# A DLRM tower on one core: ScalarE turns the ids of the first two halves into distances, VectorE compares them with constants, and the first ids are loaded ahead of the first table

## The chip, the core and the metric

The kernel runs on one core of a Trainium2 chip. The metric is the device time of a run in microseconds. The kernel before took 383.13 us (median of 3 runs, 382.71 to 384.81). What can be told about where that time goes comes from one profiled execution of the same program.

## The reference

For 2048 samples, 27 embedding rows of 128 floats are looked up, all pairs of the 27 are multiplied out, and a small network runs over the 351 dot products and 16 dense features.

```
e = stack([tbl_f[ids[:, f]] for f in range(27)], axis=1)       # 2048 x 27 x 128
dot = einsum('bnd,bmd->bnm', e, e)                             # 2048 x 27 x 27
z = dot at the 351 pairs i < j
h = concatenate([z, dense_ctx], axis=1)                        # 2048 x 367
h = maximum(h @ W_top1 + b_top1, 0)                            # 512 wide
h = maximum(h @ W_top2 + b_top2, 0)                            # 256 wide
y = h @ W_top3
```

The tables have 1000 to 125000 rows. Ten of the small ones (seven with 1000 rows, three with 1250) are read in a special way, below.

## The kernel before

**Tiles and halves.** The batch is cut into 16 tiles of 128 samples, and two neighbouring tiles make a half, so there are 8 halves (h = 0 to 7). For every tile the embeddings are needed turned, with the 128 numbers of a row on the partitions, in `embT`. There are two ways into `embT`.

**Gathered features.** GpSimd (POOL) issues one indirect DMA for each tile and feature (L379), which fetches 128 rows from the table into `emb` (three for the first two tiles into `flatT`). TensorE turns them four at a time (a "quad", L420, function `turn`) into a bank of PSUM, and ScalarE copies the bank to `embT` (`copy_quad`, L642). A tile has 20 gathered features in half 0 and 17 later, so five quads, written here as quad(t, q). There are 278 gathers in all, issued in one fixed order.

**Features read in one piece ("hots").** For the ten small tables the row is picked by a matrix product. A table lies in SBUF on 125 partitions, 8 or 10 rows (chunks) to a partition, so row r lies on partition r // c as chunk r % c, where c is 8 or 10. For each chunk VectorE builds a matrix `one_hot` of 125 x 256 zeros and ones (`build`, L537): it compares the 256 ids of a half, which were copied to all partitions as int32 (`ids`), with one number per partition, `row_of[p, chunk] = c*p + chunk`. TensorE multiplies the chunk of the table with it (`read_table`, L410) and sums over the chunks in a bank of PSUM; ScalarE copies that bank to `embT` (`copy_hot`, L634). The hots are numbered in the order of use: hot 0 to 6 are those of half 0, hot 7 to 16 those of half 1, then ten for every half, 77 in all. Each has 8 or 10 comparisons, so 658 in all; 142 of them belong to hots 0 to 16.

**The tables are split first.** A table goes into the product as a rounded part and a rest. ScalarE makes the rounded part (`split_high`, L622), and VectorE the rest (`split_low`, L522, signal `low_ready`). Tables 0 to 4 are staged in the space of `embT` for later tiles, tables 5 to 9 in the buffers `h1T`, `w2_sb` and `w1_sb` that the network's weights need later. Tables 5 and 6 are read unsplit in half 0. Tables 8 and 9 are loaded only when table 7's and 8's stage in `w1_sb` has been read by `split_low`, and the weights `W1` after table 9's.

**The queues.** Each engine runs its own list in order, and one that waits holds everything behind it. TensorE, VectorE and ScalarE all walk through one list `ORDER`. Around half 1 it reads: quad(1,0), dots of tile 0 (part 0), hot 7, quad(1,1), hot 8, quad(1,2), dots of tile 0 (part 1), hot 9, quad(1,3), hot 10, quad(1,4), hot 11, quad(2,0), dots of tile 1 (part 0), the turning of tile 0's pairs, hot 12, quad(2,1), hot 13, quad(2,2), dots of tile 1 (part 1), hot 14, quad(2,3), hot 15, quad(2,4), hot 16, quad(3,0), dots of tile 2 (L442). Three banks of PSUM go round for quads and hots: TensorE may write for one of them only when ScalarE has copied the one three places earlier (`bank_of`, waits on `embT_ready`). VectorE builds one hot ahead of TensorE's reading.

ScalarE's splits of tables 5 to 9 stand right ahead of its copies of hots 7, 8, 9, 11 and 13 (`SPLIT_AT`). VectorE's stand ahead of the build of the hot after it.

SyncE issues the loads. Four buffers `ids` go round, and the load of the ids of hot n waits until hot n-4 is built. The part of its list on which much rests here is this:

```
for n in range(EARLY, len(HOTS)):        # EARLY = 11
    load_ids(n)
    if n == EARLY:
        load_table(SHARED + 1)           # table 8: waits for low_ready 8 (table 7's)
    elif n == EARLY + 2:
        load_table(SHARED + 2)           # table 9: waits for low_ready 9 (table 8's)
        sp.wait_ge(hot_used, BEFORE[len(HOT0)])
        sp.dma_start(w2_sb...)
    elif n == EARLY + 5:
        sp.wait_ge(low_ready, O)         # then W1, W3 and b2
```

So the ids of hots 12 and 13 go out behind table 8, and those of hots 14, 15 and 16 behind table 9 and `W2`.

Of the kernel before, what the change touches and what calls it, by code (L numbers as in the profile page):

```python
# [6 lines left out]
F32 = mybir.dt.float32  # L7
# [45 lines left out]
def dlrm_tower(nc, dense, idx_rows, ids_hot, tables, w1, w2, b2, w3, y):  # L53
# [54 lines left out]
    def hots_of(h):  # L108

        return range(READ_IN_HALF[h])  # L110
# [65 lines left out]
        BEFORE.append(BEFORE[-1] + GROUPS[o])  # L176
    READ = {step: n for n, step in enumerate(HOTS)}

    EARLY = len(HOT0) + IDS

    SHARED = WHOLE + 2
# [4 lines left out]
    with ctx:  # L186
# [6 lines left out]
        def sem(name):  # L193
            return ctx.enter_context(nc.semaphore(name))
# [84 lines left out]
        staged = [sem(f"staged{o}") for o in range(O)]  # L279
        high_ready = sem("high_ready")  # L280
        low_ready = sem("low_ready")
        ids_loaded = [sem(f"ids_loaded{b}") for b in range(IDS)]
        hot_built = sem("hot_built")
        hot_used = sem("hot_used")
# [27 lines left out]
        @block.sync  # L312
        def _(sp):
            def load_ids(n):
                _, h, o = HOTS[n]
                if n >= IDS:

                    sp.wait_ge(hot_built, BEFORE[n - IDS + 1])
                src = ids_hot[o:o + 1, h * HN:(h + 1) * HN].to_broadcast([P, HN])
                sp.dma_start(ids[:, n % IDS, :], src).then_inc(ids_loaded[n % IDS], 16)  # L320

            def load_table(o):
                if o > SHARED:

                    sp.wait_ge(low_ready, o)
                rows = tables[ONE_HOT[o]].rearrange("(p c) d -> p (c d)", p=ROWS)
                for a, b in ((0, SPLIT), (SPLIT, ROWS)):
                    sp.dma_start(raw(o, a, b), rows[a:b, :]).then_inc(staged[o], 16)

            sp.dma_start(idx[:, 0, :], idx_rows[:, 0, :]).then_inc(idx_first, 16)  # L330
            for o in range(SHARED + 1):
                load_table(o)
                if o < len(HOT0):
                    load_ids(o)
                if o == 2:
                    sp.dma_start(idx[:, 1:T, :], idx_rows[:, 1:T, :]).then_inc(idx_rest, 16)
            for n in range(len(HOT0), EARLY):
                load_ids(n)
            sp.dma_start(dense_sb[:, :, :], dense).then_inc(dense_loaded, 16)
            for n in range(EARLY, len(HOTS)):  # L340
                load_ids(n)
                if n == EARLY:
                    load_table(SHARED + 1)
                elif n == EARLY + 2:
                    load_table(SHARED + 2)

                    sp.wait_ge(hot_used, BEFORE[len(HOT0)])
                    sp.dma_start(w2_sb[:, :, :], w2.rearrange("(k p) n -> p k n", p=P)).then_inc(weights_loaded, 16)
                elif n == EARLY + 5:

                    sp.wait_ge(low_ready, O)
                    sp.dma_start(w1_sb[0:KR, :, :], w1).then_inc(weights_loaded, 16)
                    sp.dma_start(w3_sb[:, :], w3.to_broadcast([P, H2])).then_inc(weights_loaded, 16)
                    sp.dma_start(b2_sb[:, :], b2.to_broadcast([P, H2])).then_inc(weights_loaded, 16)
            sp.wait_ge(y_in_rows, 1)
            sp.dma_start(y.rearrange("(t c) o -> t (c o)", c=TILE), h2[0:T, 0:TILE]).then_inc(y_stored, 16)
            sp.wait_ge(y_stored, 16)
# [161 lines left out]
        def _(dve):  # L519
# [7 lines left out]
            def build(n):  # L527
                _, _, o = HOTS[n]
                of = ids[0:ROWS, n % IDS, :]
                dve.wait_ge(ids_loaded[n % IDS], 16 * (n // IDS + 1))  # L530
                for i in range(GROUPS[o]):
                    k = BEFORE[n] + i
                    if k >= SLOTS:
                        dve.wait_ge(hot_used, k - SLOTS + 1)
                    for c in range(GROUP):
                        chunk = i * GROUP + c
                        done = dve.tensor_scalar(one_hot[0:ROWS, k % SLOTS, c, :], of,  # L537
                                                 row_of[0:ROWS, KINDS.index(CH[o]), chunk:chunk + 1], None,
                                                 ALU.is_equal)
                    done.then_inc(hot_built, 1)  # L540

            def place_dense(t):
# [75 lines left out]
        @block.scalar  # L618
        def _(act):
            def split_high(o):  # L620
                act.wait_ge(staged[o], 32)
                act.copy(tbl[0:ROWS, 0, AT[o]:AT[o + 1], :],  # L622
                         raw(o, 0, ROWS).rearrange("p (c d) -> p c d", d=D)).then_inc(high_ready, 1)

            def copy_hot(h, o):
                n = READ["hot", h, o]
                if h == 1:

                    act.wait_ge(low_ready, WHOLE)
                elif h > 1:  # L630
                    act.wait_ge(dotted, PARTS * HT * (h - 1))
                act.wait_ge(hot_used, BEFORE[n + 1])
                at = h % 2 * HT
                act.copy(embT_at(at, HT, slot(o), 1),  # L634
                         embT_ps[USE["hot", h, o] % BANKS][:, 0:HN].rearrange("p (t s q) -> p t s q", t=HT, s=SIDES),
                         ).then_inc(embT_ready, 1)

            def copy_quad(t, q):
                s = quad(t, q)
                n = len(s)  # L640
                act.wait_ge(turned, TURNED["quad", t, q])
                act.copy(embT_at(t % TB, 1, s[0], n),  # L642
                         embT_ps[USE["quad", t, q] % BANKS][:, 0:n * P].rearrange("p (f s q) -> p f s q", f=n, s=SIDES),
                         ).then_inc(embT_ready, 1)

            def copy_ring(t):

                act.wait_ge(flat_filled, 4 * t + 2)
                if t >= 2:
                    act.wait_ge(flat_turned, t - 1)  # L650
                act.copy(pairs[:, t % 2, :, 1:HALF + 1], ring()).then_inc(first_pairs, 1)  # L651

            def copy_flat(t):
                act.wait_ge(flat_turned, t + 1)
                act.copy(flatT[0:KR, :, t % HT * TILE:(t % HT + 1) * TILE],  # L655
                         flat_ps[0:KR, 0:KC * TILE].rearrange("p (k c) -> p k c", k=KC)).then_inc(flatT_ready, 1)

            def relu1(n):
                act.wait_ge(h1_summed, n + 1)
                if n == T - 1:  # L660
                    at = n % HT * TILE
                    half = C1 // 2
                    act.activation(h1T[:, 0:half, at:at + TILE],
                                   h1_ps[:, 0:half * TILE].rearrange("p (k c) -> p k c", k=half),
                                   ACT.Relu).then_inc(h1_ready, 1)
                    act.wait_ge(h1_summed, n + 2)
                    act.activation(h1T[:, half:C1, at:at + TILE],
                                   flat_ps[:, 0:half * TILE].rearrange("p (k c) -> p k c", k=half),
                                   ACT.Relu).then_inc(h1_ready, 1)
                elif n >= T - HT:  # L670
                    act.activation(h1T[:, :, n % HT * TILE:(n % HT + 1) * TILE],
                                   h1_ps[:, :].rearrange("p (k c) -> p k c", k=C1), ACT.Relu).then_inc(h1_ready, 1)
                else:
                    first = n % HT * C1 // HT
                    act.activation(h1T[:, first:first + C1 // HT, :],  # L675
                                   h1_ps[:, :].rearrange("p (k c) -> p k c", k=C1 // HT),
                                   ACT.Relu).then_inc(h1_ready, 1)

            AHEAD = 3
            for o in range(AHEAD):  # L680
                split_high(o)
            for kind, *of in ORDER:
                if kind == "hot":
                    n = READ["hot", of[0], of[1]]
                    if n + AHEAD < WHOLE:
                        split_high(n + AHEAD)
                    elif n in SPLIT_AT:
                        split_high(SPLIT_AT[n])
                if kind == "quad":
                    copy_quad(*of)  # L690
                elif kind == "hot":
                    copy_hot(*of)
                elif kind == "ring":
                    copy_ring(*of)
                elif kind == "flat":
                    copy_flat(*of)
                elif kind == "layer1":
                    relu1(*of)
# [32 lines left out]
```

## Time and profile before

| | us |
|---|---|
| median of 3 runs | 383.13 (382.71 to 384.81) |
| the profiled execution, its time | 381.17 |
| its span, first to last instruction | 379.3 |
| TensorE busy | 345.7 |
| VectorE busy | 294.4 |
| GpSimd busy | 269.3 |
| ScalarE busy | 153.3 |

The span is shorter than the execution's time by 1.9 us, which lie around it. The profiled execution is 1.96 us shorter than the median. In what follows, PE is TensorE's matmuls, PEld its loads of weights, DVE is VectorE, ACT is ScalarE, POOL is GpSimd and SP is SyncE. Buffer numbers are left out of the names, so `w_sb` is `w1_sb` or `w2_sb`.

### The profile page before, as it was taken

Reading aid. Unit: us, or ns where it says so; the run is one execution under the profiler, and the core shown is the slowest. Engines: PE = TensorE matmul, PEld = TensorE weight load, DVE = VectorE, ACT = ScalarE, POOL = GpSimd, SP = SyncE. Lnnn points to the kernel's source line nnn. Section 1 sums busy time; section 2 is a strip of 40 time slices with the busy share of each in tenths; the row PEclk is TensorE's granted clock in tenths of the full one; section 3 lists DMA queues with packets and bytes.
Section 4 is the critical chain, followed back from the end, with each engine's and each line's share of the span. In section 5 each row is a group of like instructions: output and inputs, shape, how many; then the busy total and the mean of one; then the engine's idle time right before and its main releaser. Section 6 shows DMA issues by size and latency. Waiting matters only on the chain.

```text
span 379.3 us, 9954 instructions
## 1 busy us (share of the span) xinstructions
PE 345.7 (91%) x4035; PEld 322.6 (85%) x4035; DVE 294.4 (78%) x821; ACT 153.3 (40%) x217; POOL 269.3 (71%) x287
## 2 busy tenths in 40 slices
PE   1788868599999999999999999999999999999985
PEld 1677767588999999998999999998999999998874
DVE  4986696898688969798689969798689869793432
ACT  3352644434343453534343453534243453533421
POOL 6777877777777777777777777777777777777400
PEclk9989996999999999999999999999999999999999
DMA  6995225953333333334333333333343343221100
GB/s 184 251 247 136 64 63 137 213 186 96 82 93 85 79 84 82 95 69 95 82 94 85 79 86 81 95 72 91 85 91 85 76 89 83 76 57 50 36 2 1
DMA packets 22988, 36.38 MB, mean 96 GB/s; under 512 B 6224, under 2 KB 17120, under 8 KB 22944
## 3 DMA queue, kind: packets, MB, share of 16 engines
q0 software_dynamic: 8896, 18.24, 20.2%
q1 hardware_dynamic: 14048, 17.52, 18.6%
q8 instruction: 32, 0.52, 0.5%
q14 instruction: 12, 0.10, 0.1%
HBM read 35.73 MB, written 0.01 MB: 94 GB/s over the span
## 4 chain that ended last, share of the span: by engine, by line
PE 75%; POOL 14%; issue 5%; DMA 3%; ACT 2%; DVE 1%; ACTq 0%; DVEq 0%
PE embT_ps L410 35%; PE gram_ps L442 13%; POOL emb L379 12%; PE h_ps L470 11%; PE h_ps L494 7%; PE embT_ps L420 6%; DMA emb<-in_tbl,idx 3%; PE flat_ps L453 2%; POOL flatT L379 2%; ACT embT L634 1%; DVE flat L568 1%; DMA idx<-in_idx_rows 0%; PE h_ps L481 0%; PE flat_ps L481 0%; DVE flat L569 0%
## 5 line engine op out<-in xcount | busy, mean ns | idle before, releaser
L379 POOL DMA_INDIRECT emb<-in_tbl,idx x272 | 261.8, 962 | 83.8 <-issue 80.6
L537 DVE TENSOR_SCALAR one_hot<-ids,row_of 125x256 fp32r<-125x256 int32 x658 | 205.4, 383 | 13.2 <-PE embT_ps L410 10.6
L410 PE MATMUL embT_ps<-one_hot,tbl 125*128 125x256 f32 x1284 | 182.0, 297 | 13.0 <-DVE one_hot L537 11.4
L410 PEld LDWEIGHTS embT_ps<-one_hot,tbl 125*128 125x128 f32 x1284 | 166.7, 196 | 17.9 <-issue 8.9
L634 ACT COPY embT<-embT_ps 128x256 f32<-128x256 f32 x77 | 48.0, 624 | 134.2 <-PE embT_ps L410 129.0
L642 ACT COPY embT<-embT_ps 128x512 f32<-128x512 f32 (+1 forms) x80 | 80.7, 1012 | 11.7 <-PE embT_ps L420 11.7
L568 DVE STREAM_TRANSPOSE flat<-gram_ps 128x864 f32<-128x864 f32 x31 | 33.5, 1082 | 43.7 <-PE gram_ps L442 43.1
L442 PEld LDWEIGHTS gram_ps<-embT 128*59 128x59 f32 x1984 | 56.2, 134 | 9.6 <-ACT embT L634 3.9
L442 PE MATMUL gram_ps<-embT 128*59 128x54 f32 x1984 | 60.2, 217 | 3.8 <-ACT embT L634 2.3
L420 PE MATMUL embT_ps<-ident,emb 128*128 128x128 f32 x272 | 43.8, 276 | 11.6 <-DMA emb<-in_tbl,idx 8.6
L420 PEld LDWEIGHTS embT_ps<-ident,emb 128*128 128x128 f32 x272 | 32.2, 142 | 13.8 <-DMA emb<-in_tbl,idx 11.4
L470 PE MATMUL h_ps<-flatT,w_sb 126*128 126x256 f32 (+1 forms) x192 | 42.2, 370 | 0.0
L470 PEld LDWEIGHTS h_ps<-flatT,w_sb 126*128 126x128 f32 x192 | 33.5, 190 | 4.1
L494 PE MATMUL h_ps<-w_sb,h1T 128*128 128x256 f32 x128 | 31.2, 386 | 0.2 <-ACT h1T L675 0.2
L494 PEld LDWEIGHTS h_ps<-w_sb,h1T 128*128 128x128 f32 x128 | 23.0, 190 | 3.4 <-ACT h1T L675 0.5
L675 ACT ACTIVATE h1T<-h_ps 128x512 f32<-128x512 f32 x14 | 8.4, 597 | 33.0 <-PE h_ps L470 33.0
L569 DVE STREAM_TRANSPOSE flat<-gram_ps 128x416 f32<-128x416 f32 x31 | 17.8, 573 | 0.0
L556 DVE TENSOR_TENSOR h<-h_ps,b_sb 128x256 f32<-128x256 f32 x16 | 6.7, 420 | 13.4 <-PE h_ps L494 13.4
L655 ACT COPY flatT<-flat_ps 126x384 f32<-126x384 f32 x16 | 7.8, 486 | 20.5 <-PE flat_ps L453 20.5
L651 ACT COPY pairs<-flat 128x351 f32<-128x351 f32 x16 | 13.0, 815 | 3.7 <-DVE flat L569 3.7
L576 DVE COPY_PREDICATED pairs<-second,flat 128x351 f32<-128x351 int32 x16 | 12.6, 790 | 0.6
L622 ACT CAST tbl<-embT 125x1024 fp32r<-125x1024 f32 x5 | 5.2, 1046 | 13.2 <-DMA embT<-in_tbl 13.2
(47 smaller groups left out, 85.0 us busy)
## 6 DMA issues: line engine op xcount, KB each, us to landing
ids<-in_ids_hot SPq DMA_DIRECT2D x77, 128.0 KB
emb<-in_tbl,idx POOLq DMA_INDIRECT x272, 3.1
embT<-in_tbl SPq DMA_DIRECT2D x5, 448.0 KB
w_sb<-in_tbl SPq DMA_DIRECT2D x3, 560.0 KB
w_sb<-in_W_ring SPq DMA_DIRECT2D x1, 756.0 KB
w_sb<-in_W_top SPq DMA_DIRECT2D x1, 512.0 KB
h1T<-in_tbl SPq DMA_DIRECT2D x1, 448.0 KB
w_sb<-in_tbl SPq DMA_DIRECT2D x1, 448.0 KB
```

The source lines that it names most:

```text
L379: pool.indirect_dma_start(gathered_row(t, s), None, tables[f][:, :], bass.IndirectOffsetOnAxis(ap=idx[:, t, f:f + 1], axis=0),).then_inc(g ...
L410: mm = pe.matmul(out[:, 0:HN], tbl[0:ROWS, part, AT[o] + chunk, :], one_hot[0:ROWS, k % SLOTS, c, :], start=(chunk == 0 and part == 0), st ...
L420: mm = pe.transpose(out[:, i * P:(i + 1) * P], gathered_row(t, s), ident[:, :])
L442: mm = pe.matmul(at[:, i * SLOT:i * SLOT + SIDES * FEATS].rearrange("p (s c) -> p s c", s=SIDES), embT[:, t % TB, q, :], two_samples(t, q) ...
L470: mm = pe.matmul(h1_ps[:, i * width:(i + 1) * width], w1_sb[0:KR, k, c * P:(c + 1) * P], x[:, k, :], start=(k == 0), stop=(k == KC - 1))
L494: mm = pe.matmul(h2_ps[:, :], h1T[:, k, t % HT * TILE:(t % HT + 1) * TILE], w2_sb[:, k, :], start=(k == 0), stop=(k == C1 - 1))
L537: done = dve.tensor_scalar(one_hot[0:ROWS, k % SLOTS, c, :], of, row_of[0:ROWS, KINDS.index(CH[o]), chunk:chunk + 1], None, ALU.is_equal)
L568: dve.transpose(flat[:, 0:FEATS, :], by_column(t, part, 0, FEATS)).then_inc(flat_filled, 1)
L569: dve.transpose(flat[:, FEATS:FROWS, :], by_column(t, part, 0, WRAP)).then_inc(flat_filled, 1)
L634: act.copy(embT_at(at, HT, slot(o), 1), embT_ps[USE["hot", h, o] % BANKS][:, 0:HN].rearrange("p (t s q) -> p t s q", t=HT, s=SIDES),).then ...
L642: act.copy(embT_at(t % TB, 1, s[0], n), embT_ps[USE["quad", t, q] % BANKS][:, 0:n * P].rearrange("p (f s q) -> p f s q", f=n, s=SIDES),).t ...
L651: act.copy(pairs[:, t % 2, :, 1:HALF + 1], ring()).then_inc(first_pairs, 1)
```

## The change

ScalarE gets a new step `relative_ids(n)` for the first two halves (hots 0 to 16, `RELATIVE` = 17). In place, it makes from the int32 ids the float `c*p - id` for each partition p. The value is `-chunk` where the id's row lies on this partition as that chunk. VectorE then compares the buffer, read as float32, with the constant `-chunk` in place of a number per partition; it waits for ScalarE's step and no longer for the load. For hots 17 and later nothing changes. SyncE issues the ids of hot 0 ahead of table 0.

ScalarE runs the new step of hot n+3 right ahead of its copy of hot n, and behind the split that stands there, if one does.

```diff
+    RELATIVE = len(HOT0) + len(hots_of(1))
...
             sp.dma_start(idx[:, 0, :], idx_rows[:, 0, :]).then_inc(idx_first, 16)
+            load_ids(0)
             for o in range(SHARED + 1):
                 load_table(o)
-                if o < len(HOT0):
+                if 0 < o < len(HOT0):
                     load_ids(o)
...
                 of = ids[0:ROWS, n % IDS, :]
-                dve.wait_ge(ids_loaded[n % IDS], 16 * (n // IDS + 1))
+                if n < RELATIVE:
+                    dve.wait_ge(ids_relative, n + 1)
+                else:
+                    dve.wait_ge(ids_loaded[n % IDS], 16 * (n // IDS + 1))
...
-                        done = dve.tensor_scalar(one_hot[0:ROWS, k % SLOTS, c, :], of,
-                                                 row_of[0:ROWS, KINDS.index(CH[o]), chunk:chunk + 1], None,
-                                                 ALU.is_equal)
+                        columns = one_hot[0:ROWS, k % SLOTS, c, :]
+                        if n < RELATIVE:
+                            done = dve.tensor_scalar(columns, of.bitcast(F32), float(-chunk), None, ALU.is_equal)
+                        else:
+                            done = dve.tensor_scalar(columns, of, row_of[0:ROWS, KINDS.index(CH[o]), chunk:chunk + 1],
+                                                     None, ALU.is_equal)
...
+            def relative_ids(n):
+
+                act.wait_ge(ids_loaded[n % IDS], 16 * (n // IDS + 1))
+                if n == 0:
+                    act.wait_ge(rows_ready, len(KINDS))
+                kind = KINDS.index(CH[HOTS[n][2]])
+                act.activation(ids[0:ROWS, n % IDS, :].bitcast(F32), ids[0:ROWS, n % IDS, :], ACT.Identity,
+                               bias=row_of[0:ROWS, kind, 0:1], scale=-1.0).then_inc(ids_relative, 1)
...
             AHEAD = 3
+            relative_ids(0)
             for o in range(AHEAD):
                 split_high(o)
+                if o > 0:
+                    relative_ids(o)
             for kind, *of in ORDER:
                 if kind == "hot":
...
+                    if n + AHEAD < RELATIVE:
+                        relative_ids(n + AHEAD)
                 if kind == "quad":
                     copy_quad(*of)
```

ScalarE in the kernel before, from the split of table 7 to the turned pairs of tile 0. L634 copies a hot (9, 10 and 11), L642 a quad:

```order
L622 CAST tbl<-w1_sb 125x1280 [waits staged7]
L634 COPY embT<-embT_ps 128x2x2x64 [waits hot_used,low_ready]
L642 COPY embT<-embT_ps 128x4x2x64 [waits turned]
L634 COPY embT<-embT_ps 128x2x2x64 [waits hot_used,low_ready]
L642 COPY embT<-embT_ps 128x4x2x64 [waits turned]
L622 CAST tbl<-w1_sb 125x1280 [waits staged8]
L634 COPY embT<-embT_ps 128x2x2x64 [waits hot_used,low_ready]
L642 COPY embT<-embT_ps 128x4x2x64 [waits turned]
L655 COPY flatT<-flat_ps 126x3x128 [waits flat_turned]
```

The same place in the changed kernel; L641 is the new step, for hots 12, 13 and 14 (the lines of the others are shifted by 10 or 19):

```order
L632 CAST tbl<-w1_sb 125x1280 [waits staged7]
L641 ACTIVATE ids<-ids,row_of 125x256 [waits ids_loaded0]
L653 COPY embT<-embT_ps 128x2x2x64 [waits hot_used,low_ready]
L661 COPY embT<-embT_ps 128x4x2x64 [waits turned]
L641 ACTIVATE ids<-ids,row_of 125x256 [waits ids_loaded1]
L653 COPY embT<-embT_ps 128x2x2x64 [waits hot_used,low_ready]
L661 COPY embT<-embT_ps 128x4x2x64 [waits turned]
L632 CAST tbl<-w1_sb 125x1280 [waits staged8]
L641 ACTIVATE ids<-ids,row_of 125x256 [waits ids_loaded2]
L653 COPY embT<-embT_ps 128x2x2x64 [waits hot_used,low_ready]
L661 COPY embT<-embT_ps 128x4x2x64 [waits turned]
L674 COPY flatT<-flat_ps 126x3x128 [waits flat_turned]
```

Ahead of the copies of hots 9, 10 and 11 there now stands a wait for the ids of hots 12, 13 and 14.

SyncE in the changed kernel, from the ids of hot 11 (the first row) to `W1`; this order is the same as before, only the line numbers differ:

```order
L323 DMA ids<-in_ids_hot 128x256 [waits hot_built]
L331 DMA w1_sb<-in_tbl_6 112x1280 [waits low_ready]
L331 DMA w1_sb<-in_tbl_6 13x1280
L323 DMA ids<-in_ids_hot 128x256 [waits hot_built] x2
L331 DMA w1_sb<-in_tbl_8 112x1280 [waits low_ready]
L331 DMA w1_sb<-in_tbl_8 13x1280
L352 DMA w2_sb<-in_W_top2 128x4x256 [waits hot_used]
L323 DMA ids<-in_ids_hot 128x256 [waits hot_built] x3
L356 DMA w1_sb<-in_W1_ring 126x1536 [waits low_ready]
```

Nothing moved in this piece. `in_tbl_6` is table 8 of the ten and `in_tbl_8` is table 9; the two ids between them are those of hots 12 and 13, the three behind `W2` those of hots 14, 15 and 16.

## Rows read from the trace of the kernel before

**Rows 1.** Stretch, us; busy of PE, PEld, DVE, ACT, POOL; PEclk, DMA share, GB/s

```profile
0.00:82.00 82.00, 56.69 (x561) 51.49 (x562) 62.55 (x157) 34.86 (x42) 62.09 (x69) 0.94 0.67 168
88.58:344.09 255.51, 253.55 (x3048) 240.23 (x3048) 213.56 (x619) 106.31 (x157) 193.54 (x204) 1.00 0.35 83
```

**Rows 2.** TensorE's waits from 0 to 88.58: total us, times, longest

```profile
PE embT_ps L410 <- DVE one_hot L537: 11.4, 3, 8.5
PE embT_ps L420 <- DMA emb<-in_tbl,idx: 8.6, 6, 2.9
```

**Rows 3.** TensorE's waits from 88.58 to 344, all of them

```profile
PE gram_ps L442 <- ACT embT L634: 1.9, 6, 0.3
```

**Rows 4.** TensorE's timeline, 53 to 92: start, length, what [idle before]

```profile
55.62 3.04 PE L410 MATMUL embT_ps<-one_hot,tbl 125*128 125x256 f32 x16 [1.99 <-DVE one_hot L537]
...
60.26 0.47 PE L420 MATMUL embT_ps<-ident,emb 128*128 128x128 f32 x1 [1.60 <-DMA flatT<-in_tbl,idx]
...
70.38 0.66 PE L420 MATMUL embT_ps<-ident,emb 128*128 128x128 f32 x4 [1.21 <-DMA emb<-in_tbl,idx]
70.80 2.16 PE L410 MATMUL embT_ps<-one_hot,tbl 125*128 125x256 f32 x16
75.83 0.66 PE L420 MATMUL embT_ps<-ident,emb 128*128 128x128 f32 x4 [2.88 <-DMA emb<-in_tbl,idx]
...
78.29 2.65 PE L410 MATMUL embT_ps<-one_hot,tbl 125*128 125x256 f32 x20
81.35 0.66 PE L420 MATMUL embT_ps<-ident,emb 128*128 128x128 f32 x4 [0.41 <-DMA emb<-in_tbl,idx]
81.77 2.83 PE L410 MATMUL embT_ps<-one_hot,tbl 125*128 125x256 f32 x20
...
87.66 0.60 PE L420 MATMUL embT_ps<-ident,emb 128*128 128x128 f32 x4
```

**Rows 5.** ScalarE's timeline, 50 to 64

```profile
50.12 1.30 ACT L622 CAST tbl<-w_sb 125x1280 fp32r<-125x1280 f32 x1
53.28 0.61 ACT L634 COPY embT<-embT_ps 128x256 f32<-128x256 f32 x1 [1.86 <-PE embT_ps L410]
53.68 1.10 ACT L642 COPY embT<-embT_ps 128x512 f32<-128x512 f32 x1
...
62.26 1.28 ACT L622 CAST tbl<-w_sb 125x1280 fp32r<-125x1280 f32 x1
```

**Rows 6.** SyncE's timeline, 53 to 80

```profile
54.97 0.77 SPq L328 DMA_DIRECT2D w_sb<-in_tbl  x2
55.79 0.82 SPq L320 DMA_DIRECT2D ids<-in_ids_hot  x2
65.10 0.79 SPq L328 DMA_DIRECT2D w_sb<-in_tbl  x2
```

**Rows 7.** DMA queue 1: packets, MB, share; first from 54.9 to 59.6

```profile
q1 hardware_dynamic: 350, 0.83, 72.7%
```

**Rows 8.** The same queue from 65 to 71.5

```profile
q1 hardware_dynamic: 861, 1.33, 78.7%
```

**Rows 9.** VectorE's timeline, 63 to 92

```profile
63.58 1.50 DVE L522 TENSOR_TENSOR tbl<-w_sb,tbl 125x1280 fp32r<-125x1280 f32 x1 [3.70 <-ACT tbl L622]
...
78.41 1.08 DVE L568 STREAM_TRANSPOSE flat<-gram_ps 128x864 f32<-128x864 f32 x1 [0.67 <-PE gram_ps L442]
...
80.75 8.78 DVE L537 TENSOR_SCALAR one_hot<-ids,row_of 125x256 fp32r<-125x256 int32 x28
```

**Rows 10.** GpSimd's timeline, 40 to 47: two issues of gathers

```profile
41.65 0.94 POOL L379 DMA_INDIRECT emb<-in_tbl,idx  x1 [0.30 <-issue]
42.89 2.00 POOL L379 DMA_INDIRECT emb<-in_tbl,idx  x1 [0.30 <-issue]
```

**Rows 11.** VectorE's timeline at the same place

```profile
42.86 1.21 DVE L522 TENSOR_TENSOR tbl<-h1T,tbl 125x1024 fp32r<-125x1024 f32 x1
```

More of the change, by code:

```diff
@@ L281, in dlrm_tower @@
         low_ready = sem("low_ready")
+        ids_relative = sem("ids_relative")
         ids_loaded = [sem(f"ids_loaded{b}") for b in range(IDS)]
```

## The prediction

> **What bounds the kernel now.** I read first the busy time by stretch. From 0 to 82 us TensorE works 57 of 82 us; from 88.58 to 344.09 it works 253.6 of 255.5 [rows 1], and its only waits there are six of 0.3 us [rows 3]. So the kernel has two regimes: a start in which TensorE waits for others, and a long stretch in which it is the bound and keeps its own pace, so that whatever it is late at 88.58 it is late at the end. The change works on hots 0 to 16 only, all in the start. The question is when quad(3,0) runs, at 87.66 before [rows 4].
>
> Then I read what TensorE waits for in the start: 11.4 us for one-hot matrices, of which 8.5 are the very first wait, so 2.9 us later, the last of them before 55.62 [rows 4]; and 8.6 us for gathered rows in six waits [rows 2]. The timeline puts the gather waits last: quad(1,4) waits 1.60 us and starts at 60.26, quad(2,1) starts at 70.38, quad(2,2) at 75.83, quad(2,3) at 81.35, each after a DMA [rows 4]. They come at the pace of GpSimd's issues, 0.94 us and 0.30 us between them [rows 10]. A faster VectorE doesn't bring them forward. The 2.9 us lie ahead of them and are taken up by them.
>
> **The change, part by part.**
>
> *VectorE's comparison.* In a long row 28 comparisons take 8.78 us [rows 9], (8.78 - 0.34) / 27 = 0.313 us from one start to the next, for 256 elements. That is one element per cycle or so, with about 0.05 us on top. No row has a comparison of float32 with a constant. Bounds: unchanged 0.313, or two elements at a time, 0.13 + 0.05 = 0.19. I take 0.19, because both things that differ, the int32 input and the number per partition, are gone. 142 comparisons then save 142 x 0.12 = 17 us of VectorE's time, nearly all of it beside waits for gathers. What shows is the row from hot 15 to quad(3,0): 87.66 - 81.77 = 5.9 us before [rows 4], where VectorE paced hot 16, and 5.25 at TensorE's own pace.
>
> The page "Vector Engine (DVE) Microarchitecture Reference", section 5.1, in the Trainium skill, names no dtype in its condition for two elements per cycle over two ports, only SBUF on both sides and an even count. By it the old int32 form would already run at about 0.19; this trace says 0.313, and the measurement decides.
>
> *ScalarE's 17 new steps.* Nearest row: a copy of 256 columns takes 0.61 us and the next starts 0.40 after it [rows 5]. I take 0.45 each, 0.4 to 0.6 as bounds. ScalarE has room for the 7.7 us (35 of 82 us busy [rows 1]). What counts is where the step waits.
>
> *The wait for the ids of hot 12.* It stands ahead of the copy of hot 9, which ran at 53.28 [rows 5]. SyncE issues those ids only behind table 8, at 55.79, and table 8 only at 54.97, when VectorE's split of table 7 is done [rows 6]. Table 8 is 0.64 MB, one set of ids 0.13 MB; the queue had moved 0.83 MB by 59.6 [rows 7], so the ids of hot 12 are there at about 59.5, and signalled near 60.0. The step ends at 60.45, the copy of hot 9 at 61.05. Quad(1,4) needs that bank: 61.1 for 60.26, +0.85. Behind it stand the copy of quad(1,3), the step for hot 13, the copies of hot 10 and quad(1,4) (0.90 + 0.45 + 0.40 + 0.90; 0.90 is my reading of a quad's copy of 1.10 [rows 5], whose last 0.2 lies beside the next), so the split of table 8 starts at 63.5 for 62.26 [rows 5]: +1.2. VectorE's split follows (63.58 before [rows 9]), and SyncE sends table 9 at 66.3 for 65.10 [rows 6].
>
> *The wait for the ids of hot 14.* It stands ahead of the copy of hot 11. The ids go out behind table 9 (0.64 MB) and W2 (0.52 MB), 1.29 MB with themselves; from 65 to 71.5 the queue moved 1.33 MB [rows 8]. So they were there at about 71.4, signalled at 71.9, and now at 73.1. ScalarE does nothing from 64.8 to 73.1. The step ends at 73.55, the copy of hot 11 at 74.15. Quad(2,1), which needs its bank, starts at 74.2 for 70.38. Hot 13 needs the bank of quad(2,0), copied at 75.05, and takes 2.0: quad(2,2) at 77.1 for 75.83 [rows 4].
>
> *The end of the start.* ScalarE has a backlog: copies of quad(2,0), of tile 0's pairs and of hot 12, the ring copy, quad(2,1), and the step for hot 15 (0.90 + 0.40 + 0.45 + 0.40 + 0.70 + 0.90 from 73.95), so its split of table 9 runs from 77.7 to 79.0, and VectorE's to 80.5. Only then is hot 14 built: 80.95 for 78.29. It takes 2.5, so quad(2,3) is at 83.45. VectorE ends the build at 82.4, needs 80.75 - 78.41 = 2.34 us for the transposes and pairs of tile 1 [rows 9], and has hot 15's first pair at 85.15. TensorE reads hots 15 and 16 in 5.25: quad(3,0) at 90.45. 90.45 - 87.66 = **+2.8 us**.
>
> *The first ids ahead of table 0.* 0.13 MB more ahead of the first table delay the first product (8.5 us) by 0.4 to 0.7 us, and ScalarE's waits for the ids of hots 5 to 7, each behind a table, delay copies by some 2 us. Both end at quad(0,3), whose gather was late anyway (among the waits of rows 2): nothing.
>
> *What two-port comparisons do to GpSimd.* A gather's issue that starts at 42.89 takes 2.00 us in place of 0.94 [rows 10], while VectorE runs a subtraction of two SBUF tensors from 42.86 to 44.07 [rows 11]: the issue stood still until it ended, and went on for its usual rest. A comparison that takes two elements at a time needs two reads per cycle too. Up to 43 us there are 31 gathers and 72 comparisons (hots 0 to 8), 72 x 0.19 = 13.7 us, a third of the time: ten issues meet one and lose half of 0.19. Bounds: nothing, and, if an issue gets in only when a whole run of eight has ended, 9 runs x 0.75 = 6.8 us. I take **+1.0**, near the lower bound, since the seen loss ended with one instruction. Each microsecond of it delays the split of table 7 and all above.
>
> The page "SBUF — State Buffer" of the Trainium skill, "two separate sides", says that a VectorE instruction in a two-port mode shuts GpSimd out of writing its DMA descriptors until it ends. The long issue agrees for a two-input instruction; no row shows a two-port mode.
>
> Sum: 2.8 + 1.0 = 3.8 us. On the profiled execution 381.17 + 3.8 = 385.0; on the median, 1.96 higher, **386.9**.
>
> **The rivals.**
>
> *The comparison stays at 0.313.* Then no port is contended, but the start ends later: hot 14 at 81.15, its build ends at 83.6, with 2.34 and a pair 86.6, and twenty comparisons at 0.313 pace hots 15 and 16: quad(3,0) at 92.85, +5.2, 388.3. For it: int32 and float32 are equally wide. Against it: both differences are gone at once. 0.13.
>
> *Runs of comparisons keep GpSimd out whole.* 2.8 + 6.8 = 9.6, 392.7. For it: the comparisons follow each other without a gap. Against it: a new arbitration at each. 0.12.
>
> *ScalarE's waits stay off TensorE's path.* If the ids of hot 14 land by 69.3 or so in place of 73.1, copies run as before, the gathers set the start, nothing changes: 383.1. Against it: the megabytes of rows 8. 0.15.
>
> *Faster.* VectorE's saving arrives: the 2.9 us of waits and the 0.65 at hot 16, 3.5 us, 379.6. It decides if gathers land earlier than I read, and ScalarE isn't held. Against it: four gather waits after the last one-hot wait [rows 4]. 0.10.
>
> **How the numbers follow.** The forecast has 0.50, with 385.2 to 389 as its own spread. My range leaves out the faster case and the upper half of the 392.7 case: 382.6 to 392.0. Within 0.5% (381.2 to 385.05, about what a measurement can tell from no change): 0.15 and 0.05 from the forecast's low edge, 0.20. Faster 0.10, slower 0.70.
>
> **What would show it.** ScalarE idle for some 8 us before the step at 60 and some 8 us before 73, both put down to the loads of ids; quad(2,1) near 74 for 70.38; quad(3,0) at 90 to 92; a comparison every 0.19 us up to about 88; more issues above 0.94 us; and the stretch from quad(3,0) to the end as long as before. I am wrong if ScalarE's gap at 65 to 73 is under 4 us, if TensorE's lateness at quad(3,0) isn't there at the end, or if GpSimd's issues stretch by over 4 us.

## The result, and the profile after

| | before | after |
|---|---|---|
| median of 8 runs each | 383.06 (380.39 to 384.81) | 386.64 (384.77 to 389.93) |
| profiled execution, its span | 381.17, 379.3 | 384.77, 383.0 |

The ratio after to before is 1.0125, with a 95% interval of 1.0084 to 1.0165. The forecast was 386.9. Both profiled executions lie 1.9 us below their medians, the one after being the fastest of its eight. The time came out as forecast; the sum behind it did not, and most of what follows is on that.

TensorE's timeline of the kernel after, at the places of [rows 4] (start, length, instructions, idle time before and what ended it):

```profile
61.45 0.45 PE L424 MATMUL embT_ps<-ident,emb 128*128 128x128 f32 x1 [3.09 <-ACT embT L653]
...
75.08 1.09 PE L424 MATMUL embT_ps<-ident,emb 128*128 128x128 f32 x4 [3.98 <-ACT embT L653]
75.87 3.78 PE L414 MATMUL embT_ps<-one_hot,tbl 125*128 125x256 f32 x16
79.45 1.01 PE L424 MATMUL embT_ps<-ident,emb 128*128 128x128 f32 x4
...
82.26 2.66 PE L414 MATMUL embT_ps<-one_hot,tbl 125*128 125x256 f32 x20
...
86.30 2.62 PE L414 MATMUL embT_ps<-one_hot,tbl 125*128 125x256 f32 x20 [0.94 <-DVE one_hot L546]
...
91.26 0.60 PE L424 MATMUL embT_ps<-ident,emb 128*128 128x128 f32 x4
```

These are quad(1,4), quad(2,1), hot 13, quad(2,2), hot 14, hot 15 and quad(3,0). Where TensorE waited for a gathered row before, it now waits for a copy of ScalarE, and quad(3,0) starts at 91.26 for 87.66: 3.6 us late. The stretch behind it, from the dots of tile 2 at 92.18 (88.58 before), is the one of [rows 1] again, the same 3048 matmuls in the same 255.51 us:

```profile
92.18:347.69 255.51, 253.54 (x3048) 240.21 (x3048) 213.68 (x618) 106.36 (x157) 193.24 (x205) 1.00 0.34 83
```

So what the start lost is lost at the end: 3.6 us at quad(3,0), 3.7 in the span. ScalarE's timeline says who held it:

```profile
60.32 0.51 ACT L641 ACTIVATE ids<-ids,row_of 125x256 f32<-125x256 int32 x1 [9.00 <-DMA ids<-in_ids_hot]
60.73 0.57 ACT L653 COPY embT<-embT_ps 128x256 f32<-128x256 f32 x1
...
63.68 1.26 ACT L632 CAST tbl<-w_sb 125x1280 fp32r<-125x1280 f32 x1
73.94 0.51 ACT L641 ACTIVATE ids<-ids,row_of 125x256 f32<-125x256 int32 x1 [9.00 <-DMA ids<-in_ids_hot]
...
78.39 1.28 ACT L632 CAST tbl<-w_sb 125x1280 fp32r<-125x1280 f32 x1
```

Two idle stretches of 9.00 us stand ahead of the steps for hots 12 and 14, both ended by the load of their ids. Behind the first stands the copy of hot 9 (53.28 in [rows 5], now 60.73), and at its end the split of table 8 (62.26, now 63.68). SyncE's list shows why the ids come late. They are issued behind a table, and the table behind VectorE's split of the one before:

```profile
54.88 0.77 SPq L331 DMA_DIRECT2D w_sb<-in_tbl  x2
55.70 0.82 SPq L323 DMA_DIRECT2D ids<-in_ids_hot  x2
66.50 0.78 SPq L331 DMA_DIRECT2D w_sb<-in_tbl  x2
67.31 0.40 SPq L352 DMA_DIRECT2D w_sb<-in_W_top  x1
67.75 1.58 SPq L323 DMA_DIRECT2D ids<-in_ids_hot  x3
```

VectorE's timeline gives the end of the start:

```profile
79.70 1.49 DVE L526 TENSOR_TENSOR tbl<-w_sb,tbl 125x1280 fp32r<-125x1280 f32 x1 [7.67 <-ACT tbl L632]
81.11 2.35 DVE L546 TENSOR_SCALAR one_hot<-ids 125x256 fp32r<-125x256 f32 x10
83.38 1.06 DVE L578 STREAM_TRANSPOSE flat<-gram_ps 128x864 f32<-128x864 f32 x1
...
85.66 4.48 DVE L546 TENSOR_SCALAR one_hot<-ids 125x256 fp32r<-125x256 f32 x20
```

The split of table 9 waited 7.67 us for ScalarE; then the ten comparisons of hot 14, the transposes, and the first pair of hot 15, on which TensorE waited until 86.30. A comparison now starts every (2.35 - 0.30) / 9 = 0.23 us, 0.313 before.

**Which runs say what.** Three of the kernels below ran on chips on which the kernel before takes 381.5 to 382.9 us. The nine others ran on chips on which it took 565 to 577 us itself, with its engines standing still for 5 to 10 us at a time from some 17 us on, so no ratio comes from those: used from them is only how long single instructions took, and what happened before the first standstill.

### The profile page after: what moved, and what is told of

Same layout as the page of the kernel before. It is cut to its first block, busy times and chain, and to the rows that moved or that the text cites. A ratio compares the mean times of both kernels' runs of the same rounds, so it can differ in the third digit from the quotient of the medians.

```text
span 383.0 us, 9972 instructions
## 1 busy us (share of the span) xinstructions
PE 345.5 (90%) x4035; PEld 323.7 (85%) x4035; DVE 283.0 (74%) x821; ACT 158.9 (41%) x234; POOL 270.1 (71%) x287
## 4 chain that ended last, share of the span: by engine, by line
PE 75%; POOL 8%; issue 4%; DMA 4%; ACT 4%; DVE 3%; ACTq 0%; DVEq 0%
PE embT_ps L414 35%; PE gram_ps L446 14%; PE h_ps L474 11%; POOL emb L383 8%; PE h_ps L498 7%; PE embT_ps L424 6%; DMA ids<-in_ids_hot 3%; PE flat_ps L457 2%; ACT embT L653 2%; DVE one_hot L546 1%; DMA emb<-in_tbl,idx 1%; ACT embT L661 1%; DVE flat L578 1%; POOL flatT L383 1%; ACT tbl L632 1%
## 5 line engine op out<-in xcount | busy, mean ns | idle before, releaser
L548 DVE TENSOR_SCALAR one_hot<-ids,row_of 125x256 fp32r<-125x256 int32 x516 | 160.5, 383 | 9.2 <-PE embT_ps L414 9.2
L546 DVE TENSOR_SCALAR one_hot<-ids 125x256 fp32r<-125x256 f32 x142 | 33.6, 303 | 7.2 <-PE embT_ps L414 3.5
L641 ACT ACTIVATE ids<-ids,row_of 125x256 f32<-125x256 int32 x17 | 8.5, 503 | 23.3 <-DMA ids<-in_ids_hot 23.3
L526 DVE TENSOR_TENSOR tbl<-w_sb,tbl 125x1280 fp32r<-125x1280 f32 (+1 forms) x4 | 5.7, 1427 | 15.0 <-ACT tbl L632 15.0
```

The costliest lines, as they stand in the source:

```text
L546: done = dve.tensor_scalar(columns, of.bitcast(F32), float(-chunk), None, ALU.is_equal)
L548: done = dve.tensor_scalar(columns, of, row_of[0:ROWS, KINDS.index(CH[o]), chunk:chunk + 1], None, ALU.is_equal)
```

## The experiments

Two costs were in the forecast: ScalarE's waits for ids, and comparisons with constants that hold GpSimd's issues up. The changed kernel has both. The plan was to take away the one, the other, and both.

### The waits taken away, the comparisons with constants kept

```
-                    if n + AHEAD < RELATIVE:
+                    if n + AHEAD < 12:
                         relative_ids(n + AHEAD)
+                    if 12 <= n + 1 < RELATIVE:
+                        relative_ids(n + 1)
```

> The same kernel as e1_steps_late, on another chip: the changed kernel with the steps for hots 12 to 16 ahead of the copy of the hot one place earlier, not three. Theory (copies of PSUM banks queued behind a step that waits for ids): no idle stretch of 9 us before the step for hot 12, under 2 us before that for hot 14, quad(2,1) near 70.4, quad(3,0) near 87.5, 0.998 to 1.002 of the kernel before. Rival (two-port comparisons hold GpSimd up, or the 17 steps cost by themselves): 1.003 or above with the waits gone. Rival (the comparisons are a gain that the waits had hidden): 0.99.

Measured: 384.15 us (382.37 to 385.21, 12 runs) against 382.85 for the kernel before on the same chip, ratio 1.0034 (1.0013 to 1.0055). The median lies above the 0.998 to 1.002 of the theory, at the 1.003 of the rival that comparisons or steps cost by themselves, and the interval reaches into both. By the medians about a quarter of the loss stays. ScalarE and TensorE of this kernel:

```profile
64.14 0.51 ACT L641 ACTIVATE ids<-ids,row_of 125x256 f32<-125x256 int32 x1
76.51 0.50 ACT L641 ACTIVATE ids<-ids,row_of 125x256 f32<-125x256 int32 x1
```

```profile
61.42 0.33 PE L424 MATMUL embT_ps<-ident,emb 128*128 128x128 f32 x1 [2.55 <-DMA flatT<-in_tbl,idx]
...
73.33 1.11 PE L424 MATMUL embT_ps<-ident,emb 128*128 128x128 f32 x4 [3.11 <-DMA emb<-in_tbl,idx]
...
83.83 0.66 PE L424 MATMUL embT_ps<-ident,emb 128*128 128x128 f32 x4 [1.79 <-DMA emb<-in_tbl,idx]
...
90.13 1.94 PE L446 MATMUL gram_ps<-embT 128*59 128x54 f32 x64 [0.31 <-ACT embT L653]
```

The steps for hots 12 and 14 run with no idle time ahead of them: both waits are gone. But the quads wait for gathered rows, longer than before: quad(1,4) is at 61.42 for 60.26, quad(2,1) at 73.33 for 70.38, quad(2,3) at 83.83 for 81.35, and the dots of tile 2 at 90.13 for 88.58, +1.55. Quad(2,1) near 70.4 and quad(3,0) near 87.5 were expected; they came at 73.33 and 89.22. (In the long stretch this execution lost 0.9 us more. On this chip 28 comparisons of the old kind take 8.70 us and not 8.57; the kernel before wasn't traced on it, so that this is the chip's own is argued, not shown.)

### Both taken away, and the waits alone

The comparison's form was set back by giving VectorE the same numbers from a tile, one per partition, in place of constants:

```
+        minus = sb("minus", [P, max(CH)])
...
+            for c in range(max(CH)):
+                dve.memset(minus[:, c:c + 1], float(-c))
...
-                            done = dve.tensor_scalar(columns, of.bitcast(F32), float(-chunk), None, ALU.is_equal)
+                            done = dve.tensor_scalar(columns, of.bitcast(F32), minus[0:ROWS, chunk:chunk + 1], None, ALU.is_equal)
```

With the steps in their later places this is the first kernel below, with the steps as in the change the second.

> Both suspected costs taken away: the steps of hots 12 to 16 in the later places of e1b_steps_late (no wait of 9 us), and VectorE comparing the float32 distances with a number per partition as in e5_float_pointer (0.31 us each, no GpSimd issue stretched by one). The 17 steps and the early first ids stay. If e1b's rest of +1.3 us is contention with GpSimd: gone here but for the slower builds, quad(2,1) near 70.4 to 71, quad(3,0) at 87.7 to 88.3, 1.000 to 1.002. Rival (the steps themselves or the early ids cost it): 1.003 or above again, the first 52 issues of GpSimd summing to 52.6 us and not 54.1 to 54.8.

> The same kernel as e5_float_pointer on another chip: the places and waits of the change, comparisons with a number per partition at 0.31 us. If ScalarE's two waits are the larger cost and lie on another path than GpSimd's issues: 1.010 to 1.014, as much as the whole change, quad(2,1) near 74.5 to 75 after ScalarE's wait, quad(3,0) at 91 to 92. If the two costs add up (waits 2.3 us, contention 1.3): 1.005 to 1.008.

Measured, both on one chip, where the kernel before took 381.49: neither cost 381.70 (381.13 to 384.52), ratio 1.0015 (0.9992 to 1.0038), which can't be told from no change; the waits alone 388.05 (385.34 to 389.13), ratio 1.0152 (1.0119 to 1.0184). The first is the 1.000 to 1.002 expected, with quad(3,0) at 88.24 as expected too, quad(2,1) at 71.75 a little later. The second is above the 1.010 to 1.014 expected: quad(2,1) came at 76.04 for 74.5 to 75 and quad(3,0) at 95.01 for 91 to 92.

GpSimd's issues from 0 to 77 us, grouped (count, busy us, mean ns), of the kernel before, of that with neither cost, and of that with only the constants (e1b):

```profile
L379 POOL DMA_INDIRECT emb<-in_tbl,idx x50 | 50.8, 1015 | 16.0 <-issue 14.6 <-DMA idx<-in_idx_rows 1.1 <-PE embT_ps L420 0.3
L379 POOL DMA_INDIRECT flatT<-in_tbl,idx x6 | 6.5, 1089 | 1.8 <-issue 1.8
```

```profile
L384 POOL DMA_INDIRECT emb<-in_tbl,idx x50 | 50.7, 1014 | 15.9 <-issue 14.9 <-DMA idx<-in_idx_rows 0.9
L384 POOL DMA_INDIRECT flatT<-in_tbl,idx x6 | 6.8, 1135 | 1.8 <-issue 1.8
```

```profile
L383 POOL DMA_INDIRECT emb<-in_tbl,idx x49 | 51.8, 1056 | 15.7 <-issue 14.6 <-DMA idx<-in_idx_rows 1.0
L383 POOL DMA_INDIRECT flatT<-in_tbl,idx x6 | 5.9, 977 | 1.8 <-issue 1.8
```

57.3 us for 56 issues, 57.5 for 56, and 57.7 for 55; the 56th of the last, from 77.16 on, takes 1.79 us, so that it ends at 78.95, in the kernel with neither cost at 76.97. That is 2.0 us, but the constants are only half of it. In all five undisturbed traces an issue that starts more than 0.02 us after one of the long subtractions (`split_low`), while it runs, ends 0.82 us after the subtraction's end, where that is later than 0.94 us after its own start: 42.89 + 2.00 is 44.89, and the subtraction ends at 44.07 [rows 10] [rows 11]. One that starts at most 0.02 us after the subtraction, or ahead of it, isn't held by it. So each issue's length can be taken apart, for issues 2 to 56:

| kernel | held by subtractions, us | the rest over 0.94 us each |
|---|---|---|
| before | 4.1 | 0.1 |
| neither cost | 4.3 | 0.3 |
| waits alone | 2.5 | 0.1 |
| constants alone | 5.1 | 1.3 |
| both (the change) | 3.7 | 1.1 |

The second column is what goes with the constants, 1.0 us or so: 14 issues of 0.99 to 1.04 us. The first column goes by where a subtraction's start falls between two issues. It differs by 1.8 us between two kernels with the same comparison, and no run here ties it to the constants.

ScalarE of the kernel with the waits alone, then its VectorE, then its TensorE:

```profile
60.52 0.51 ACT L644 ACTIVATE ids<-ids,row_of 125x256 f32<-125x256 int32 x1 [9.15 <-DMA ids<-in_ids_hot]
...
74.91 0.51 ACT L644 ACTIVATE ids<-ids,row_of 125x256 f32<-125x256 int32 x1 [9.73 <-DMA ids<-in_ids_hot]
```

```profile
82.08 3.05 DVE L547 TENSOR_SCALAR one_hot<-ids,minus 125x256 fp32r<-125x256 f32 x10
```

```profile
88.10 3.91 PE L415 MATMUL embT_ps<-one_hot,tbl 125*128 125x256 f32 x20 [1.74 <-DVE one_hot L547]
```

The waits are those of the change, and hot 15 starts at 88.10 for 86.30, again after VectorE. The table puts the four together. The third column is when the dots of tile 2 start (88.58 before), the last what one median is over the other.

| waits | comparison | dots of tile 2 | ratio to before |
|---|---|---|---|
| no | per partition | 89.16 (+0.6) | 1.0015 (0.9992 to 1.0038) |
| no | constant | 90.13 (+1.6) | 1.0034 (1.0013 to 1.0055) |
| yes | per partition | 95.92 (+7.3) | 1.0152 (1.0119 to 1.0184) |
| yes (the change) | constant | 92.18 (+3.6) | 1.0125 (1.0084 to 1.0165) |

The two costs don't add. Without the waits the start goes by the gathers, and the kernel with constants is 1.0 us later in the traces (90.13 against 89.16), with the subtractions' part in it. With the waits it goes by ScalarE and VectorE, nobody waits for a late gather, and the traces differ by 3.7 us the other way. Of that, 1.0 is not the comparison's: the ids of hot 14 came that much earlier in the one execution (73.94, 74.91). The rest is the comparison's: hot 14's ten comparisons take 2.35 us and not 3.05, the twenty behind them 4.48 and not 6.28. By the medians the gain is less, 0.3% of 383 or 1 us; the trace of the change is of its fastest execution, that of the waits alone of one 0.4 us above its median. Both of these differences between medians lie inside the intervals of the ratios, so their sizes rest on one trace each. The difference that the waits make, 0.9% with constants and 1.4% without, is outside them. That the costs don't add is likewise read from the traces: a plain sum of the two (1.0152 + 1.0034 - 1.0015 = 1.017) can't be told from 1.0125 by these intervals.

### Which difference makes the comparison fast

One kernel kept int32 ids (ScalarE's step writes them) and the constants, the other float32 and a number per partition. Both ran on disturbed chips, so only the lengths count.

> The changed kernel with ScalarE's step writing the distance as int32, and VectorE comparing int32 ids with the same constants: one of the two differences between the old and the new comparison is left. Places, waits and queues as changed. If int32 is what held the old comparison at 0.313 us: 0.31 here, no GpSimd issue of 1.02 to 1.2 us beside a comparison, and the time is that of ScalarE's waits alone with slower builds of hots 14 to 16, 1.010 to 1.016. If the number per partition held it: 0.22 here, issues stretched as in the changed kernel, 1.010 to 1.014. What tells them apart is the time per comparison and GpSimd's issues; the sum of the first 52 issues was 52.6 us before, 54.1 changed.

> The changed kernel with the float32 distances kept and VectorE comparing them with a number per partition (a tile of -chunk, written once at the start) in place of a constant. Places, waits and queues as changed. If the number per partition held the old comparison at 0.313 us: 0.31 here and GpSimd's issues not stretched by comparisons; ScalarE's two waits of 9 us stay and the time says what they cost alone, 1.010 to 1.016. If int32 held it: 0.22 here and issues stretched, 1.010 to 1.014.

VectorE's first run of eight and two of GpSimd's issues, of the one (with the subtraction that the first issue meets) and of the other:

```profile
9.91 1.82 DVE L546 TENSOR_SCALAR one_hot<-ids 125x256 fp32r<-125x256 int32 x8
```

```profile
12.44 1.24 POOL L383 DMA_INDIRECT emb<-in_tbl,idx  x1 [0.30 <-issue]
13.98 1.03 POOL L383 DMA_INDIRECT emb<-in_tbl,idx  x1 [0.30 <-issue]
```

```profile
11.65 1.21 DVE L526 TENSOR_TENSOR tbl<-embT,tbl 125x1024 fp32r<-125x1024 f32 x1
```

```profile
9.95 2.52 DVE L547 TENSOR_SCALAR one_hot<-ids,minus 125x256 fp32r<-125x256 f32 x8
```

```profile
12.40 0.95 POOL L384 DMA_INDIRECT emb<-in_tbl,idx  x1 [0.31 <-issue]
13.65 0.95 POOL L384 DMA_INDIRECT emb<-in_tbl,idx  x1 [0.30 <-issue]
```

int32 with a constant takes (1.82 - 0.26) / 7 = 0.22 us from start to start, float32 with a number per partition (2.52 - 0.34) / 7 = 0.31. It is the number per partition that held the old comparison, not int32. The fast form is also the one beside which an issue takes 1.03 us for 0.94. The 1.24 isn't its doing: that issue ends at 13.68, 0.82 after the subtraction that ran from 11.65 to 12.86. The medians were 586.14 and 581.47 us beside 576.65 for the kernel before: no verdict.

### The first ids ahead of table 0, alone

```
+            load_ids(0)
             for o in range(SHARED + 1):
                 load_table(o)
-                if o < len(HOT0):
+                if 0 < o < len(HOT0):
```

> The kernel before with one part of the change: the ids of hot 0 are loaded ahead of table 0. Comparisons and ScalarE's list as before. Both theories: the first product moves by 0.4 to 0.7 us at most, and the gather waits at quad(0,3) and after it take that up; 0.999 to 1.001. If it is over 1.003, part of the loss belongs to this part of the change.

574.62 us beside 576.94: no verdict. The first microseconds are undisturbed. ScalarE's first split, VectorE's and the first product, in the kernel before and then in this one:

```profile
5.47 1.04 ACT L622 CAST tbl<-embT 125x1024 fp32r<-125x1024 f32 x1 [3.45 <-DMA embT<-in_tbl]
```

```profile
8.52 6.30 PE L410 MATMUL embT_ps<-one_hot,tbl 125*128 125x256 f32 x32 [8.52 <-DVE one_hot L537]
```

```profile
7.61 1.04 ACT L623 CAST tbl<-embT 125x1024 fp32r<-125x1024 f32 x1 [5.59 <-DMA embT<-in_tbl]
```

```profile
10.67 6.31 PE L411 MATMUL embT_ps<-one_hot,tbl 125*128 125x256 f32 x32 [10.67 <-DVE tbl L523]
```

The table is 2.14 us later, and so is the first product. In the changed kernel quad(0,0) is only 0.5 us late (16.59 for 16.08) and the dots of tile 0 0.8 us (40.08 for 39.32): the gather waits took it up, as in the kernel with neither cost, which holds this part too and measured 1.0015 (0.9992 to 1.0038).

### On disturbed chips: the other way to remove the waits, and three more

| kernel | this | before beside it |
|---|---|---|
| steps late (first try) | 576.09 | 576.94 |
| ids sent ahead of tables 8 and 9 (first try, second try) | 574.78, 568.22 | 576.94, 564.54 |
| steps and constants for hots 0 to 11 only | 577.38 | 576.94 |
| before, split cut into pieces | 573.46 | 564.54 |
| before, with constants for hots 14 to 16 only | 567.11 | 564.54 |

The kernel with the altered order of SyncE moves two lines:

```
                 load_ids(n)
-                if n == EARLY:
+                if n == EARLY + 2:
                     load_table(SHARED + 1)
-                elif n == EARLY + 2:
+                elif n == EARLY + 4:
                     load_table(SHARED + 2)
```

> The same kernel as e2_ids_before_tables on another chip: the changed kernel, with SyncE sending the ids of hots 12 and 13 ahead of table 8, and those of hots 14 and 15 ahead of table 9 and W2. ScalarE's list and the comparisons with constants as changed. If the waits for ids are the larger cost however they are removed, this equals e1b_steps_late: 1.002 to 1.006, ScalarE's idle stretches put down to ids under 2 us, quad(2,1) at 73 at the latest, the rest put down to gathers. If the place of the steps costs by itself: 1.008 or above.

ScalarE's steps as a group (count, busy and mean, idle before), of the kernel after and of this one:

```profile
L641 ACT ACTIVATE ids<-ids,row_of 125x256 f32<-125x256 int32 x17 | 8.5, 503 | 23.3 <-DMA ids<-in_ids_hot 23.3
```

```profile
L641 ACT ACTIVATE ids<-ids,row_of 125x256 f32<-125x256 int32 x17 | 8.6, 509 | 1.4 <-DMA ids<-in_ids_hot 1.4
```

The waits are gone, but everything else on that chip was late too and gave the loads time, so whether this order does it on a quiet chip stays open. The two kernels made to beat both were these:

> The kernel before with one edit: VectorE's split of a table is cut into subtractions of two chunks each (256 elements, 4 or 5 to a table) in place of one of 1024 or 1280. Four of the first 56 issues of GpSimd took 1.8 to 2.0 us before, each beside one long subtraction. If an issue that is held up goes on when the instruction ends, each loses 0.3 and not 1 us, some 3 us less by issue 55, and the gathers that TensorE waits for come earlier: 0.993 to 0.998. If it is held up until VectorE leaves such work altogether, or the gathers' landing and not their issue sets the start: 0.999 to 1.002.

> The kernel before with the change made for hots 14 to 16 only, where VectorE paced TensorE at hot 16 and no gather is waited for any more: their steps stand ahead of the copy of the hot one place earlier, the first ids stay behind table 0, and 112 comparisons stay as before. Theory: the lateness at quad(3,0) falls by the 0.65 us that hot 16 took over TensorE's own pace, less what stretched issues at 77 to 79 us take: 0.997 to 1.000. If it is 1.003 or above, the steps or the last 30 comparisons cost by themselves.

The first subtraction and the issue beside it fall ahead of the standstills. GpSimd in the kernel before, in that with pieces, and in the last, whose subtraction is whole:

```profile
6.69 1.98 POOL L379 DMA_INDIRECT emb<-in_tbl,idx  x1 [0.30 <-issue]
```

```profile
6.67 1.01 POOL L379 DMA_INDIRECT emb<-in_tbl,idx  x1 [0.30 <-issue]
```

```profile
6.71 1.84 POOL L382 DMA_INDIRECT emb<-in_tbl,idx  x1 [0.31 <-issue]
```

Cut in four, the subtraction let the issue through in 1.01 us; the four take 1.43 us and the one 1.23. The issue ends at 7.68, ahead of the last of the four, so it was held by a piece and not by all:

```profile
6.45 1.43 DVE L523 TENSOR_TENSOR tbl<-embT,tbl 125x256 fp32r<-125x256 f32 x4 [3.48 <-ACT tbl L624]
```

What that is worth in the whole kernel, and whether constants at the last three hots gain anything, isn't known: no version here is shown to beat the kernel before.

## Why the prediction was right, point by point

**Two regimes: right.** The lateness at 92.18 is that of the end, and the stretch between has its 253.5 of 255.5 us again.

**The comparison: right in kind, 0.22 to 0.23 for 0.19.** What comes on top of the forecast's 0.13 us is nearer 0.09 than 0.05. The reason given, that both differences are gone at once, was half wrong: int32 doesn't matter. The rival that it stays at 0.313 fell. The kernel built to have it, the waits alone, was 6.6 us over the kernel before, where the rival said 5.2.

**The wait for the ids of hot 12: right.** Forecast, measured: step ends 60.45, 60.8; quad(1,4) 61.1, 61.45; split of table 8 63.5, 63.68; table 9 sent 66.3, 66.50.

**The wait for the ids of hot 14: right, 0.8 us short.** The step was to start at 73.1 and started at 73.94, since the ids went out 0.2 us later and took longer to come. Quad(2,1) was to be at 74.2 and was at 75.08.

**The end of the start: the term that was mis-sized.** 2.8 us were forecast, 3.6 measured. Along VectorE's chain: the split of table 9 on ScalarE 78.39 for 77.7, what is left there of the 0.8 us from the ids of hot 14; hot 14's comparisons 2.35 for 1.9 us; hot 15's first product 86.30 for 85.15. TensorE then gave 0.35 back. Hot 13 at 3.78 us, for 2.16 before [rows 4], looks like a cost of its own. TensorE had stood for 3.98 us just before it (75.08), and from 75 to 80 us the granted clock (third number from the end) was 0.50, the lower of its two levels, 1.2 GHz. From 60 to 80 us it was 0.90 in the kernel before and 0.67 in this one:

```profile
60.00:80.00 20.00, 15.65 (x209) 14.80 (x210) 13.98 (x33) 9.17 (x11) 15.41 (x16) 0.90 0.71 177
```

```profile
60.00:80.00 20.00, 14.56 (x130) 13.87 (x131) 6.82 (x21) 10.68 (x18) 15.37 (x16) 0.67 0.58 136
75.00:80.00 5.00, 4.92 (x23) 4.85 (x24) 0.30 (x1) 5.00 (x9) 3.78 (x4) 0.50 0.39 106
```

But VectorE worked without a gap from 79.70 until the first pair of hot 15, and ScalarE from 73.94 until the split of table 9, so neither waited for TensorE there, and hot 15 waited for VectorE. The slow stretch lay beside that chain and cost nothing.

**The first ids ahead of table 0: the effect right, the size wrong.** The first product is 2.0 us later, not 0.4 to 0.7. Nothing of it was left at 48.45, where the quad that waits for a gather stands at 48.54 before.

**GpSimd: the step that failed.** +1.0 us was added to the waits. The stretched issues are there, and those that go with the comparisons come to 1.0 us or so by the 56th, though seven of them and not ten lie in the first 43 us, each losing about 0.09. The reading that a held issue goes on when the instruction ends was right. With the subtractions' part the 56th issue ends 0.6 us later than before (77.45 for 76.85). But in the changed kernel TensorE's last wait for a gather is at 48.45, its waits at quad(1,4) and quad(2,1) are for ScalarE, and VectorE's split of table 7, on which the added delay was to ride, wasn't late at all (it started at 53.45 before):

```profile
53.35 1.50 DVE L526 TENSOR_TENSOR tbl<-w_sb,tbl 125x1280 fp32r<-125x1280 f32 x1
```

A microsecond on a path that nobody waits for costs nothing. The sum was therefore 3.6 + 0, not 2.8 + 1.0, and 386.9 for 386.64 owes its closeness to two errors of opposite sign, which is luck. The sentence "each microsecond of it delays the split of table 7 and all above" is the one that the profile contradicts.

**The faster kernel: excluded for the reason given.** Four gather waits followed the last one-hot wait; with the waits for ids removed, gathers set the start, and the faster comparisons gained nothing there that the medians show.

**The two other rivals: fell.** Runs of comparisons don't keep GpSimd out whole (1.0 us for the 6.8 of that rival), and ScalarE had the ids of hot 14 at 73.94, not by 69.3.

## What to carry to other kernels

A step that is put on an idle engine brings its wait along: look at what is queued behind it in that engine's list, and whether the data it waits for is sent behind something large. Here the kernel with all 17 steps of 0.5 us but without the two waits of 9 us can't be told from the kernel before. Two costs found in a profile may be added only if they lie on the same path. Before adding one, name the wait that it makes longer: here nobody waited for the late gathers once ScalarE was the later of the two.

## What was not expected of the hardware

- A comparison with a constant takes 0.22 us for 256 elements, with a number per partition 0.31, for float32 and int32 alike.
- An issue of GpSimd beside a run of fast comparisons took 0.99 to 1.04 us for 0.94: it loses 0.1 at most, not the length of the run. That fits one comparison: 0.22 + 0.82 = 1.04.
- Whether a long subtraction holds an issue up goes by which started first. In the five undisturbed traces all 21 issues that started 0.03 to 0.66 us after one took 1.50 to 2.09 us, each ending 0.81 to 0.83 us after it. All 41 that started ahead of one, or within 0.02 us after, and overlapped it took at most 1.03. In the kernel before that is four of ten subtractions (the issues at 6.69, 42.89, 53.94 and 73.69).
- 0.13 MB sent ahead of the first table, one row of ids read for all partitions, delayed it by 2.1 us. At the 219 GB/s that the queue and the gathers moved in the first 20 us of the kernel before they would have cost 0.6, an estimate.
